# Top-k attention kernel: chunk maxima stored rank by rank, a smaller candidate list, and the small selection steps moved between chunks

## What is computed

```python
scores = jnp.einsum('bhnd,bhmd->bhnm', q, k) * DHEAD ** (-0.5)
kth = jax.lax.top_k(scores, TOPK)[0][..., -1:]
masked = jnp.where(scores >= kth, scores, jnp.finfo(scores.dtype).min)
attn = jax.nn.softmax(masked, axis=-1)
o = jnp.einsum('bhnm,bhmd->bhnd', attn, v)
```

## Time and profile before

| what | time |
|---|---|
| median of 3 runs | 5313.2 us |
| the profiled execution | 5306.6 us |
| its span | 5304.8 us |
| VectorE busy in the span | 4384.5 us (83%) |
| TensorE busy | 4161.1 us (78%) |
| ScalarE busy | 4144.0 us (78%) |
| GpSimd busy | 1502.1 us (28%) |

### The profile page before, as it was taken

One profiled execution on the slowest core, in us unless ns is written; L12 is line 12 of the kernel. 1 busy time (PEld: TensorE's weight loads), 2 busy tenths in 40 slices (PEclk: granted clock), 3 DMA queues, 4 the chain that ended last, 5 costly groups with the idle time before them and its releaser, 6 DMA issues. The chain is left out here.

```text
span 5304.8 us, 112543 instructions
## 1 busy us (share of the span) xinstructions
PE 4161.1 (78%) x32161; PEld 2808.6 (53%) x32161; DVE 4384.5 (83%) x25258; ACT 4144.0 (78%) x6082; POOL 1502.1 (28%) x362
## 2 busy tenths in 40 slices
PE   8576477776777557767777667798999999999997
PEld 4344345444444334444454445443567777777774
DVE  4899999998999899999999999430378888888885
ACT  2798599988998678988999889544268888888884
POOL 0354354444454334444454445100100000000000
PEclk9677677777777777777777777899799999999999
DMA  5000000000000000000000000100320101111012
GB/s 208 6 17 16 5 16 8 18 16 7 18 17 16 7 15 8 17 16 8 17 17 9 17 16 8 56 8 6 143 77 25 34 24 33 33 25 34 24 33 89
DMA packets 79566, 154.52 MB, mean 29 GB/s; under 512 B 8120, under 2 KB 49464, under 8 KB 73528
## 3 DMA queue, kind: packets, MB, share of 16 engines
q1 hardware_dynamic: 78904, 146.72, 9.8%
HBM read 99.50 MB, written 47.19 MB: 28 GB/s over the span
## 5 line engine op out<-in xcount | busy, mean ns | idle before, releaser
L539 POOL TENSOR_TENSOR a_probs<-a_scores,a_probs 128x2304 f32<-128x2304 f32 x288 | 1460.1, 5092 | 1778.5 <-ACT a_probs L462 1778.5
L557 DVE MAX8 a_top<-a_scores 128x8 f32<-128x36 f32 x18432 | 1830.8, 179 | 46.8 <-ACT a_scores L446 46.1
L373 PE MATMUL a_ps_t<-ident,a_probs 128*128 128x128 f32 x5184 | 973.7, 325 | 704.0 <-ACT a_probs_t L457 570.1
L373 PEld LDWEIGHTS a_ps_t<-ident,a_probs 128*128 128x128 f32 x5184 | 672.6, 164 | 992.2 <-ACT a_probs_t L457 708.6
L462 ACT ACTIVATE a_probs<-a_scores,a_steep_kth 128x2304 f32<-128x2304 f32 x290 | 641.2, 2211 | 295.0 <-DVE a_minus_max L667 295.0
L1117 PE MATMUL b_ps_t<-ident,b_soft 128*128 128x128 f32 x5184 | 744.1, 279 | 20.9 <-issue 19.3
L1242 DVE TENSOR_SCALAR_CACHE_REDUCE b_soft<-b_ps_s 128x2304 f32<-128x2304 f32 x288 | 735.2, 2553 | 26.9 <-PE b_ps_s L1101 9.0
L457 ACT ACTIVATE a_probs_t<-a_ps_t 128x512 f32<-128x512 f32 (+1 forms) x1440 | 727.2, 545 | 20.4 <-PE a_ps_t L373 7.4
L1117 PEld LDWEIGHTS b_ps_t<-ident,b_soft 128*128 128x128 f32 x5184 | 581.0, 141 | 204.0 <-issue 80.4
L1199 ACT ACTIVATE b_soft<-b_soft,b_minus_max 128x2304 f32<-128x2304 f32 x288 | 638.1, 2216 | 43.6 <-issue 26.0
L450 ACT ACTIVATE a_probs<-a_probs,a_minus_max 128x2304 f32<-128x2304 f32 x288 | 638.0, 2215 | 28.6 <-issue 18.5
(11 more groups left out here) (128 smaller groups left out, 4216.7 us busy)
## 6 DMA issues: line engine op xcount, KB each, us to landing
a_k_stack<-k_parts SPq DMA_DIRECT2D x72, 288.0 KB, 6.0
b_k_stack<-k_parts SPq DMA_DIRECT2D x72, 288.0 KB, 6.1
a_q_ring<-q_parts SPq DMA_DIRECT2D x294, 64.0 KB
b_q_ring<-q_parts SPq DMA_DIRECT2D x294, 64.0 KB
k_parts<-p_high SPq DMA_DIRECT2D x36, 256.0 KB, 2.1
k_parts<-p_rest SPq DMA_DIRECT2D x36, 256.0 KB, 2.2
q_parts<-p_high SPq DMA_DIRECT2D x36, 256.0 KB, 2.0
q_parts<-p_rest SPq DMA_DIRECT2D x36, 256.0 KB, 2.0
```

Of the source, the lines that this page charges most:

```text
L373: last = pe.transpose(ps_t[(NTG * s + g) % 2][:, P * m:P * m + P], probs[s % 2][:, P * (m0 + m):P * (m0 + m) + P], cst["ident"][:, :])
L539: pool.tensor_tensor(probs[u][:, :], scores_all[:, 2 * (p % 2) + u, :], probs[u][:, :], ALU.subtract).then_inc(masked_ready, 1)
L557: last = dve.max(top8[s // 2 % 2][:, s % 2, c, :], scores_all[:, s % 4, CHUNK * c:CHUNK * c + CHUNK])
```

## The change

The 8 maxima of a chunk are written 64 numbers apart, so that all chunks' rank 0 lie together, then all rank 1, and so on, behind the 8 rests. The candidates are then 200 numbers in a row (8 rests and ranks 0 to 2), with no filler. The rests are taken from ranks 3 to 6 (256 numbers), since rank 7 is looked at through its maximum anyway. The reduction for the extremes becomes four MAX8 over 64 numbers. The subtraction that gave the place is gone: the picked number is found by comparing the count with a list of counts. On ScalarE the same numbers are read, now without gaps. The correction of the guess is issued at c == 4, the guess at c == 8, the rest of select at c == 11 and hand_on at c == 23.

```diff
--- before.py
+++ after.py
@@ -46,6 +46,7 @@
 KEEP = 3
 REST = 8
 ROUNDS = TOPK // 8
+CANDIDATES = REST + KEEP * CHUNKS
 WINDOW = 24
@@ -286,16 +287,16 @@
         probs = [sb(f"probs{n}", [P, N]) for n in range(2)]
         probs_t = sb("probs_t", [P, MCH, P])
         scratch = sb("scratch", [P, N])
-        top8 = [sb(f"top8{n}", [P, 2, CHUNKS + REST, 8]) for n in range(2)]
-        below = sb("below", [P, 2, (CHUNKS + REST) * KEEP])
+        top8 = [sb(f"top8{n}", [P, 2, REST + 8 * CHUNKS]) for n in range(2)]
+        below = sb("below", [P, 2, CANDIDATES])
         best, eight = sb("best", [P, 2, WINDOW]), sb("eight", [P, 8])
         kth, bound = sb("kth", [P, 2]), sb("bound", [P, 1])
-        weighted, compared = sb("weighted", [P, 2, CHUNKS, 2]), sb("compared", [P, 2, CHUNKS, KEEP])
+        weighted, compared = sb("weighted", [P, 2, 2 * CHUNKS]), sb("compared", [P, 2, KEEP * CHUNKS])
         minus_first, balance = sb("minus_first", [P, 2]), sb("balance", [P, 2])
         factor, guess = sb("factor", [P, 2]), sb("guess", [P, 2])
-        above_guess, place = sb("above_guess", [P, 2]), sb("place", [P, 2])
-        places, picked = sb("places", [P, WINDOW]), sb("picked", [P, 2, WINDOW])
-        extremes, beyond = sb("extremes", [P, 2, 2]), sb("beyond", [P, 2])
+        above_guess = sb("above_guess", [P, 2])
+        counts, picked = sb("counts", [P, WINDOW]), sb("picked", [P, 2, WINDOW])
+        extremes, beyond = sb("extremes", [P, 2, 2, 8]), sb("beyond", [P, 2])
         doubt = sb("doubt", [P, 2])
         flag, flag_t, flags = sb("flag", [P, D]), sb("flag_t", [P, D]), sb("flags", [1, P])
         any_doubt, any_above = sb("any_doubt", [1, 3], I32), sb("any_above", [1, 1], I32)
@@ -474,10 +475,10 @@
                 act.wait_ge(tops_taken, 2 * pair + u + 1)
-                act.activation(weighted[:, u, :, :], top8[parity][:, u, 0:CHUNKS, 0:2], ACT.Identity,
+                act.activation(weighted[:, u, :], top8[parity][:, u, REST:REST + 2 * CHUNKS], ACT.Identity,
                                scale=-FIRST_GUESS / CHUNKS, accum_out=minus_first[:, u:u + 1]).then_inc(first_guessed, 1)
                 act.wait_ge(first_guessed, 2 * pair + u + 1)
-                act.activation(compared[:, u, :, :], top8[parity][:, u, 0:CHUNKS, 0:KEEP], ACT.Sign,
+                act.activation(compared[:, u, :], top8[parity][:, u, REST:CANDIDATES], ACT.Sign,
                                bias=minus_first[:, u:u + 1], accum_out=balance[:, u:u + 1]).then_inc(balance_ready, 1)
             def finish(s, h, pair):
@@ -554,46 +555,54 @@
                 wait_alone(dve, scores_kept, tile + 1)
                 for c in range(CHUNKS):
-                    last = dve.max(top8[s // 2 % 2][:, s % 2, c, :], scores_all[:, s % 4, CHUNK * c:CHUNK * c + CHUNK])
+                    last = dve.max(top8[s // 2 % 2][:, s % 2, REST + c:REST + c + 7 * CHUNKS + 1:CHUNKS], scores_all[:, s % 4, CHUNK * c:CHUNK * c + CHUNK])
                     if c < CHUNKS - 1:
                         between(c)
                 last.then_inc(tops_taken, 1)
+            rank = lambda tops, u, r, n=1: tops[:, u, REST + r * CHUNKS:REST + (r + n) * CHUNKS]
             def prepare(pair, tops):
-                wait_alone(dve, tops_taken, 2 * pair + 1)
-                counted(dve.max(tops[:, 0, CHUNKS:CHUNKS + REST, 0], tops[:, 0, 0:CHUNKS, KEEP:8]))
-                wait_alone(dve, tops_taken, 2 * pair + 2)
-                counted(dve.max(tops[:, 1, CHUNKS:CHUNKS + REST, 0], tops[:, 1, 0:CHUNKS, KEEP:8]))
-                counted(dve.tensor_reduce(extremes[:, :, :], tops[:, :, 0:CHUNKS, 0:8:7].rearrange("p u c k -> p u k c"),
-                                          AX.X, ALU.max))
-            def select(pair, tops):
-                candidates = lambda u: tops[:, u, :, 0:KEEP]
-                below_of = lambda u: below[:, u, :].rearrange("p (c k) -> p c k", k=KEEP)
+                for u in range(2):
+                    wait_alone(dve, tops_taken, 2 * pair + u + 1)
+                    counted(dve.max(tops[:, u, 0:REST], rank(tops, u, KEEP, 7 - KEEP)))
+                for u in range(2):
+                    for n, r in enumerate((0, 7)):
+                        counted(dve.max(extremes[:, u, n, :], rank(tops, u, r)))
+            def correct_guess(pair):
                 after(at["n"])
                 dve.wait_ge(balance_ready, 2 * pair + 2)
-                factors = counted(dve.tensor_scalar(factor[:, :], balance[:, :], -STEP / 2,
-                                                    -(1.0 + STEP * (CHUNKS * KEEP / 2 - AIM)), ALU.mult, ALU.add))
+                return counted(dve.tensor_scalar(factor[:, :], balance[:, :], -STEP / 2,
+                                                 -(1.0 + STEP * (CHUNKS * KEEP / 2 - AIM)), ALU.mult, ALU.add))
+            def guess_of(factors):
                 after(factors)
-                guesses = counted(dve.tensor_tensor(guess[:, :], factor[:, :], minus_first[:, :], ALU.mult))
+                return counted(dve.tensor_tensor(guess[:, :], factor[:, :], minus_first[:, :], ALU.mult))
+            def select(tops, guesses):
+                candidates = lambda u: tops[:, u, 0:CANDIDATES]
                 after(guesses)
                 written = [0, 0]
                 for u in range(2):
-                    rows = counted(dve.tensor_scalar(below_of(u), candidates(u), guess[:, u:u + 1], None, ALU.is_ge,
+                    rows = counted(dve.tensor_scalar(below[:, u, :], candidates(u), guess[:, u:u + 1], None, ALU.is_ge,
                                                      ALU.add, accum_out=above_guess[:, u:u + 1]))
-                counted(dve.tensor_tensor(beyond[:, :], extremes[:, :, 1], tops[:, :, CHUNKS + REST - 1, 0], ALU.max))
+                counted(dve.tensor_tensor(beyond[:, :], extremes[:, :, 1, 0], tops[:, :, REST - 1], ALU.max))
                 after(rows)
                 for u in range(2):
-                    written[u] = counted(dve.scalar_tensor_tensor(below_of(u), candidates(u), guess[:, u:u + 1],
+                    written[u] = counted(dve.scalar_tensor_tensor(below[:, u, :], candidates(u), guess[:, u:u + 1],
                                                                   candidates(u), ALU.is_lt, ALU.mult))
-                counted(dve.tensor_scalar(place[:, :], above_guess[:, :], -1.0, TOPK - 1.0, ALU.mult, ALU.add))
                 for r in range(WINDOW // 8):
                     found = [0, 0]
                     for u in range(2):
@@ -606,7 +615,7 @@
                                                                    below[:, u, :], LOWEST))
                 for u in range(2):
                     after(found[u])
-                    picked_u = counted(dve.scalar_tensor_tensor(picked[:, u, :], places[:, :], place[:, u:u + 1],
+                    picked_u = counted(dve.scalar_tensor_tensor(picked[:, u, :], counts[:, :], above_guess[:, u:u + 1],
                                                                 best[:, u, :], ALU.is_equal, ALU.mult,
                                                                 accum_out=kth[:, u:u + 1]))
                 after(picked_u)
@@ -664,23 +673,27 @@
                                 rounds_again(parity, u)
                     dve.drain()
                 dve.tensor_scalar(steep_kth[parity][:, :], kth[:, :], STEEP, None, ALU.mult)
-                dve.tensor_scalar(minus_max[parity][:, :], extremes[:, :, 0], -SCALE, None,
+                dve.tensor_scalar(minus_max[parity][:, :], extremes[:, :, 0, 0], -SCALE, None,
                                   ALU.mult).then_inc(kth_ready, 1)
             dve.memset(flag[:, :], 0.0)
-            for n in range(2):
-                dve.memset(top8[n][:, :, CHUNKS:CHUNKS + REST, 1:KEEP], LOWEST)
             for n in range(WINDOW):
-                last = dve.memset(places[:, n:n + 1], float(n))
+                last = dve.memset(counts[:, n:n + 1], TOPK - 1.0 - n)
             last.then_inc(buffers_set, 1)
             dve.wait_ge(buffers_set, 1)
             def pair_step(pair, tile, p, before=True):
+                found = {}
                 def between(c):
-                    if c == 7 and before:
-                        select(pair - 1, top8[(p - 1) % 2])
-                    if c == 19 and before:
+                    if c == 4 and before:
+                        found["factors"] = correct_guess(pair - 1)
+                    if c == 8 and before:
+                        found["guesses"] = guess_of(found["factors"])
+                    if c == 11 and before:
+                        select(top8[(p - 1) % 2], found["guesses"])
+                    if c == 23 and before:
                         hand_on(pair - 1, (p - 1) % 2)
                 chunk_tops(tile, 2 * p, between)
@@ -694,7 +707,7 @@
                     pair_step(h * HEAD_PAIRS + p, h * HEAD_TILES + 2 * p, p)
             for p in range(2, HEAD_PAIRS):
```

(2 more changed lines are left out.)

## The result

The changed kernel takes 5806.4 us (median of 6 runs, 5803.6 to 5811.7), the kernel before 5314.4 (6 runs). The ratio is 1.0929, with a 95% interval of 1.0915 to 1.0943: 492 us slower. The forecast was 5310 us, no change, in a range of 5292 to 5334. It was wrong by a wide margin.

A forecast was written before the change was run, and what follows sets the result against it. Bound: the loop kth, penalty(0), GpSimd, ScalarE up to keep_any, register load, branch, 20.50 us a pair. Only ScalarE's reads counted: 5306.6 - 3 = 5303.6, the median standing 6.6 higher, so 5310 us, range 5292 to 5334.

The forecast's parts named there:

- step (4): hand_on at c == 23: register load meets the same any_ready, price 0, bounds +26 us and -14 us.
- step (2): Rests from 256 instead of 320 numbers, -0.14 us a pair; extremes by four MAX8, 0 to -0.09; off the loop, 0.
- dear writes: Rival: MAX8's spread-out writes cost VectorE +1.09 us a pair, 74 us slower, 5384 us; 5%.
- The loop and its two sides: Loop kth, penalty(0), GpSimd, ScalarE to keep_any, register load, branch, 20.50 us a pair; select a side branch with slack.
- The 17 ns for sixteen candidates: Step (1): sixteen candidates fewer save 17 ns in each of 14 VectorE operations, 0.24 us a pair, on the side branch.
- The set-apart steps: Step (3): small steps of select set apart take 0.84 us instead of 0.40, +0.44 us from balance_ready to the first count.
- +0.13: Net delay of the doubts on the side branch, in us a pair: +0.44 from (3) less 0.31 from (1); taken to cost nothing.
- The 0.14 us of latency: Time a TensorE count needs to reach ScalarE, read at finish (L401 end to L486 start); gives the slack's lower end.
- the slack: Time the doubt count can be later before it delays ScalarE's keep_any: 0.09 us as lower end, 0.23 as upper.
- the sign of them: What would show dear writes: L557 at 187 ns or more, instead of near 179 ns and 0.098 us a chunk.
- ScalarE's reads: Step (6): 128 and 192 numbers read without gaps, 0 to 0.08 us; 0.02 us a pair taken, -3 us in all.
- The branch gap: Gap from keep_any's end to L666, 0.98 or 1.30 us by pair; in step (4) taken as 0, between -14 and +26 us.

The follow-up runs named there:

- the two mirrored runs: Changed kernel with rests from five ranks (3 to 7) again: 5315.8 us, ratio 1.0018; kernel before with rests from four ranks (3 to 6): 5790.5 us, ratio 1.0904.
- five ranks: Changed kernel with rests taken from ranks 3 to 7 instead of 3 to 6: 5315.8 us against 5305.8 for the kernel before, ratio 1.0018.
- short repair: Kernel before, with one pass picking the right kth where 64 to 71 numbers lie above, full search only beyond: 5252.4 us against 5312.7, ratio 0.9882.

## Why the prediction was wrong

**The step that failed** is the first part of the change's own description, "the rests are taken from ranks 3 to 6, since rank 7 is looked at through its maximum anyway", together with the half sentence "the other 17 ran the repair", to which step (4) gave no price. In the sum the rests stand in step (2), priced by their work alone (-0.14 us a pair, off the loop, 0) and not by what leaving a rank out does to the result. What stood at 0 there measured 11 x 44.2 = 486 us. And "ran the repair" is only half true of the kernel before: 17 pairs ran the count, and two of them the search. The doubts do stay the same ones, 19 counts in both. But a doubt has two outcomes. Before, rank 7 was both in the test and among the candidates. A row whose chunk held eight of the 64 largest was doubted, counted and found right, for about 8 us; only nine in a chunk, or more than eight in all beyond the third of their chunks, made kth wrong. After, eight are enough, and the tile pays 44 us more. 17 of the 19 tiles were right before, 6 of them still are. That the tiles moved are those with rank 7 in play follows from the two mirrored runs (one rank more or less, in either kernel, moves exactly eleven); the single rows weren't looked at.

No rival held it either. All of them were prices of work that each pair does, and the widest, dear writes, gave 74 us. The rows for it were there: x16 at L644 and L646, 41.0 and 40.7 us, say that two tiles cost over 80 us in these two instructions alone.

**What held.** The loop and its two sides: neither the shorter work of VectorE nor the shift of select moved the pairs, as the kernels without the search show (0.3 us apart; the 7 pairs fewer with the long gap hide 2 us at most). The 17 ns for sixteen candidates (373 to 356). The set-apart steps: 0.84 us to L599, the doubts 0.10 us later where I had +0.13, the time from the count to keep_any eaten down to 0.10 us, which still holds the 0.04 us that a count needs, and the two runs with a later select, of which 0.12 us of delay cost nothing and 0.51 us cost 41. The 0.14 us of latency taken from the row of finish was too long, so the slack was 0.19 us and not 0.09. Rests: 483 to 410 ns, where I had 68 ns less. The four MAX8 for the extremes lie ahead of a wait.

**Dear writes.** I had named 187 ns for L558 as the sign of them, and 187 ns it is (179 before). But 104 of these chunks take (10.19 - 0.19)/103 = 0.097 us each, as before (0.097 in the median of both traces): each instruction ends 8 ns later, and the next starts no later. The sign was badly chosen: a length alone doesn't tell what an engine is held. The rule of the Trainium skill on 16-byte lines ("SBUF — State Buffer", Door 1: The DMA port swizzle) would have made the writes pay; at 256 bytes apart the trace shows 8 ns of latency for it and no time.

**ScalarE's reads.** I took 0.02 us; the 128 numbers take 302 ns instead of 311 and the 192 take 455 instead of 456, so 0.01 us a pair, 1 us in all.

**The branch gap.** I took 0 between -14 and +26. It was 59 pairs instead of 44, 15 x 0.32 = +5 us. That is half of the 10 us that the change costs with five ranks. Of the other half the trace shows 2 us in the 17 pairs with a count (257.4 us from keep_any's end to steep_kth, 255.3 before). What is left, 3 us, is less than the interval of 4 to 14 leaves open.

## What to carry to other kernels

When a kernel guesses and then checks, list for each path behind the check how often it runs, what one run costs, and which data keep it rare; a change to the candidates must be held against that list before any nanosecond of the common path is counted. Here leaving out one rank of 64 numbers, worth 0.07 us a tile, cost the kernel a 44 us search eleven times. If a rare path is dear, it may be the better target: a short repair for the small miss made the kernel 1.2% faster (5252 us, the fastest here that computes everything), while nothing that was tried on the common path gave anything.

## What was not expected of the hardware

The gap between a register load with its branch and VectorE's next instruction has two lengths, 0.98 and 1.30 us behind keep_any, fixed for each place in the code. Moving the code by fifteen instructions moved the places, and a larger body under the branch went with more of them: 44 pairs of 143 before, 65 with the short repair, 36 with the search left out of the code.

MAX8 of 36 numbers with its eight results 256 bytes apart ends 8 ns later than with them side by side (187 ns long against 179), and holds the engine no longer (0.097 us in both).
